# Another order of the steps in the engines' rounds, in the first phase of a two-layer decoder kernel

## The reference

```python
x = x + attention0(layernorm(x))          # rotary-like: cos and sin of table angles, 16 heads, causal softmax
x = x + cross0(layernorm(x), ctx)         # 16 heads, scores clipped at +-10000, softmax, no mask
x = x + experts0(layernorm(x))            # router: softmax of 16 logits, argmax, place in the expert's queue
...                                       # layer 1: attention, cross attention, quantised feed-forward
```

## Time and profile before

| | us |
|---|---|
| median of 3 runs | 3380.1 (3377.64 to 3380.84) |
| the profiled execution | 3377.66 |
| its span, first to last instruction | 3375.9 |

### The profile page before, as it was taken

The page is one execution under the profiler, slowest core; times in us unless marked ns, Lnnn a source line. Parts: engine busy times, 40 slices in busy tenths (PEclk is TensorE's granted clock), DMA queues, the critical chain, the costliest instruction groups (busy, mean ns, idle before and its releaser), DMA issues. The chain is left out here.

```text
span 3375.9 us, 57669 instructions
## 1 busy us (share of the span) xinstructions
PE 3101.4 (92%) x21302; PEld 2150.3 (64%) x21302; DVE 2328.1 (69%) x4781; ACT 1799.4 (53%) x3243; POOL 1295.6 (38%) x1933
## 2 busy tenths in 40 slices
PE   3899999999999998699999786899999999999997
PEld 2566666666666665466666453576766667666764
DVE  3588888888888887242111484687888877888774
ACT  3788788888788874211111132555555555555552
POOL 4366666666666663100000351233333333333322
PEclk8899999999999999799999897999999999999998
DMA  5877777878777873333333253433433434433420
GB/s 99 149 119 107 105 109 108 112 101 110 104 107 108 108 99 48 118 117 117 117 104 123 78 168 80 64 62 58 68 60 56 62 59 67 63 56 59 62 39 13
DMA packets 291102, 301.17 MB, mean 89 GB/s; under 512 B 35243, under 2 KB 278427, under 8 KB 290821
## 3 DMA queue, kind: packets, MB, share of 16 engines
q1 hardware_dynamic: 276420, 273.41, 48.4%
q0 software_dynamic: 6144, 15.68, 1.6%
q10 hardware_dynamic: 8256, 8.39, 0.8%
HBM read 95.51 MB, written 50.40 MB: 43 GB/s over the span
## 5 line engine op out<-in xcount | busy, mean ns | idle before, releaser
L493 DVE TENSOR_REDUCE xa_mx<-bank 128x2 f32<-128x512 f32 x1024 | 670.5, 688 | 151.8 <-PE bank L483 146.5
L597 ACT ACTIVATE xa_p<-bank 128x512 f32<-128x512 f32 x1024 | 568.5, 599 | 310.6 <-PE bank L587 305.4
L608 DVE SCALAR_TENSOR_TENSOR xa_p<-xa_p,bank 128x1024 f32<-128x1024 f32 x256 | 306.6, 1217 | 38.4 <-PE bank L576 23.4
L933 POOL TENSOR_SCALAR_AFFINE_SELECT xa_p<-xa_p 128x256 f32<-128x256 f32 x512 | 201.7, 406 | 222.1 <-ACT xa_p L924 209.8
L620 PE MATMUL bank<-xa_p,xa_v 128*32 128x256 f32 x4096 | 277.3, 389 | 1.7 <-DVE xa_p L608 1.4
L924 ACT ACTIVATE xa_p<-bank 128x384 f32<-128x384 f32 x512 | 236.9, 492 | 54.3 <-PE bank L912 36.0
L1952 POOL DMA_INDIRECT sa_y<-expert_out,sa_s x64 | 70.1, 1095 | 508.2 <-POOLq L1853 482.5
L1747 ACT ACTIVATE ex_h<-bank,ex_b 128x512 f32<-128x512 f32 x64 | 44.0, 687 | 361.7 <-PE bank L1736 361.7
L1736 PE MATMUL bank<-ex_xt,ex_w 128*128 128x512 f32 x512 | 224.6, 597 | 0.7 <-ACT ex_xt L1727 0.7
L1766 PE MATMUL bank<-ex_w,ex_h 128*128 128x256 f32 x1024 | 224.0, 379 | 1.0 <-issue 0.9
L587 PE MATMUL bank<-ex_w,xa_ks 99*128 99x256 bf16 x1024 | 183.9, 277 | 30.5 <-ACT xa_p L597 22.2
(11 more groups left out here) (284 smaller groups left out, 6849.1 us busy)
## 6 DMA issues: line engine op xcount, KB each, us to landing
ex_w<-ra_parts SPq DMA_DIRECT2D x384, 128.0 KB, 6.6
xa_ks<-xa_pk SPq DMA_DIRECT2D x384, 128.0 KB, 4.6
ex_w<-in_L_ffn_W SPq DMA_DIRECT2D x32, 1024.0 KB, 7.2
xa_qs<-xa_pq SPq DMA_DIRECT2D x192, 128.0 KB, 4.7
ex_w<-xa_pq SPq DMA_DIRECT2D x192, 128.0 KB, 4.6
ra_x<-in_x SPq DMA_DIRECT2D x32, 256.0 KB, 8.1
xa_ctx<-in_ctx_t SPq DMA_DIRECT2D x64, 128.0 KB, 3.9
queue<-zeros ACTq DMA_DIRECT2D x4, 2048.0 KB, 7.9
```

Of the source, the lines that this page charges most:

```text
L493: c.nc.vector.tensor_reduce(c.xa.row_max[:, :, n], halves(c.banks[2 + n % 2]), AX.X, ALU.max).then_inc(s.max_taken, 1)
L597: c.nc.scalar.activation(c.xa.p_beside[:, n // 2 % 4, :, n % 2, :], halves(c.banks[n % 2]), ACT.Exp, scale=SCALE).then_inc(s.exp, 1)
L608: c.nc.vector.scalar_tensor_tensor(out=p, in0=p, scalar=1.0, in1=c.banks[bank][:, :].unsqueeze(1).broadcast_to([P, TC, 2 * S]), op0=ALU.mi ...
L933: c.nc.gpsimd.affine_select(out=diagonal, in_=diagonal, compare_op=ALU.is_ge, fill=0.0, base=0, pattern=[[0, TC], [1, P]], channel_multipl ...
```

## The change

The slots of the first phase are others; no step is added, dropped or changed, and the rounds keep their lengths. Much of it moves a step by one place among steps that don't touch it. In the steady round these steps stand elsewhere:

- TensorE: the rotary turn is behind cross score 1 (was behind cross score 9). Rotary sum 2 is behind the turn of the rows (was ahead), the first turn of the rotary sums is ahead of the turn of the rows. Cross values are behind max 7 (were behind max 4). Queries are ahead of max 0; floor 7 is behind the rotary values and ahead of cross sum 2.
- VectorE: the first cross normalisation is ahead of max 0 (was behind max 2). Some neighbours swap.
- ScalarE: the rotary values' copy is behind the cross floor (was behind cross exp 7); the queries' middle part behind rotary exp 1 (was behind exp 7); the high parts behind rotary exp 3 (were behind exp 1); the keys' middle part behind cross exp 10.
- GpSimd: the router's place and then the rotary power stand between masks 7 and 8 (place was ahead of mask 0, the power between the two low parts); the queries' low part is behind mask 0 (was behind mask 8); masks 14 and 15 are behind the split; the indirect rows are behind the second low part.
- SyncE: the stack of the queries goes ahead of the row of maxima; context behind the rotary stacks.

```diff
@@ pe_phase_a
-        for b, _ in due(n, period, (567,)):
+        for b, _ in due(n, period, (550,)):
             pe_ra_turn(c, b)
-        for b, k in due(n, period, (691, 696, 706, 708)):
+        for b, k in due(n, period, (691, 696, 708, 709)):
             pe_ra_sum(c, b, k)
-        for b, _ in due(n, period, (749,)):
+        for b, _ in due(n, period, (747,)):
             pe_xa_queries(c, 6, c.wx, b)
-        for b, _ in due(n, period, (757,)):
+        for b, _ in due(n, period, (763,)):
             pe_xa_values(c, 6, c.wx, b)
...
@@ dve_phase_a
-        for b, _ in due(n, period, (465,)):
+        for b, _ in due(n, period, (461,)):
             dve_xa_normalise(c, b, 0)
...
@@ act_phase_a
-        for b, _ in due(n, period, (373,)):
+        for b, _ in due(n, period, (376,)):
             act_ra_high(c, b)
-        for b, _ in due(n, period, (407,)):
+        for b, _ in due(n, period, (390,)):
             act_ra_values(c, b)
-        for b, _ in due(n, period, (485,)):
+        for b, _ in due(n, period, (477,)):
             act_xa_middle_q(c, b)
...
@@ pool_phase_a
-        for b, _ in due(n, period, (166,)):
+        for b, _ in due(n, period, (181,)):
             pool_ra_power(c, b)
-        for b, k in due(n, period, (231, 232, 234, 235, 236, 237, 238, 239, 240, 242, 243, 244, 245, 246, 247, 249)):
+        for b, k in due(n, period, (228, 230, 231, 232, 234, 235, 236, 237, 240, 241, 242, 243, 244, 245, 247, 248)):
             pool_ra_mask(c, b, k)
-        for b, _ in due(n, period, (270,)):
+        for b, _ in due(n, period, (258,)):
             pool_xa_low_q(c, b)
-        for b, _ in due(n, period, (306,)):
+        for b, _ in due(n, period, (304,)):
             pool_xa_split_both(c, b)
-        for b, _ in due(n, period, (344,)):
+        for b, _ in due(n, period, (354,)):
             pool_rt_place(c, b)
-        for b, _ in due(n, period, (345,)):
+        for b, _ in due(n, period, (369,)):
             pool_rt_rows(c, d["queue"], b)
...
```

More of the change, by code:

```diff
@@ L1322, in pe_phase_a @@
             pe_xa_turn_out(c, b)
-        for b, _ in due(n, period, (950,)):
+        for b, _ in due(n, period, (949,)):
             pe_a_project(c, 6, b)
-        for b, _ in due(n, period, (968,)):
+        for b, _ in due(n, period, (969,)):
             pe_rt_turn(c, 0, b)
-        for b, _ in due(n, period, (972,)):
+        for b, _ in due(n, period, (973,)):
             pe_rt_logits(c, 3, b)
@@ L1341, in dve_phase_a @@
             dve_ra_index(c, b)
-        for b, _ in due(n, period, (362,)):
+        for b, _ in due(n, period, (361,)):
             dve_ra_normalise(c, b, 0)
@@ L1345, in dve_phase_a @@
             dve_ra_normalise(c, b, 1)
-        for b, _ in due(n, period, (365,)):
+        for b, _ in due(n, period, (364,)):
             dve_xa_rest_k(c, 6, c.wx, b)
@@ L1353, in dve_phase_a @@
             dve_xa_normed(c, c.ra.x1[b % 4], b)
-        for b, _ in due(n, period, (382,)):
+        for b, _ in due(n, period, (383,)):
             dve_xa_rest_q(c, 6, c.wx, b)
-        for b, k in due(n, period, (420, 421, 422, 425, 426, 427, 428, 430, 431, 432, 433, 434, 435, 436, 437, 438)):
+        for b, k in due(n, period, (421, 422, 423, 425, 426, 427, 428, 430, 431, 432, 433, 434, 435, 436, 437, 438)):
             dve_xa_max(c, b, k)
@@ L1359, in dve_phase_a @@
             dve_xa_bound(c, b)
-        for b, k in due(n, period, (446, 448, 449, 453, 455, 458, 459, 460)):
+        for b, k in due(n, period, (447, 448, 449, 453, 455, 458, 459, 460)):
             dve_xa_clip(c, b, 2 * k)
-        for b, _ in due(n, period, (465,)):
+        for b, _ in due(n, period, (461,)):
             dve_xa_normalise(c, b, 0)
@@ L1367, in dve_phase_a @@
             dve_a_end(c, 6, b)
-        for b, _ in due(n, period, (484,)):
+        for b, _ in due(n, period, (485,)):
             dve_rt_stats(c, b)
@@ L1377, in act_phase_a @@
     period = ROUND_A["act"]
-    for n in range((B - 1) * period + 620):
-        for b, _ in due(n, period, (358,)):
+    for n in range((B - 1) * period + 618):
+        for b, _ in due(n, period, (355,)):
             act_ra_xn_t(c, b)
@@ L1414, in act_phase_a @@
             act_xa_raw(c, b, 0)
-        for b, _ in due(n, period, (579,)):
+        for b, _ in due(n, period, (580,)):
             act_xa_raw(c, b, 1)
@@ L1420, in act_phase_a @@
             act_rt_xn_t(c, 0, b)
-        for b, _ in due(n, period, (619,)):
+        for b, _ in due(n, period, (617,)):
             act_rt_exp(c, b)
@@ L1460, in sp_phase_a @@
     period = ROUND_A["sp"]
-    for n in range((B - 1) * period + 63):
-        for b, _ in due(n, period, (3,)):
+    for n in range((B - 1) * period + 68):
+        for b, _ in due(n, period, (2,)):
             sp_ra_load(c, x_rows[b], b)
-        for b, _ in due(n, period, (20,)):
+        for b, _ in due(n, period, (23,)):
+            sp_ra_stack(c, b, 0)
+        for b, _ in due(n, period, (24,)):
+            sp_ra_stack(c, b, 1)
+        for b, _ in due(n, period, (25,)):
             sp_xa_context(c, d["ctx_t"][b], b)
[L1466 to L1469, removed]
+        for b, _ in due(n, period, (36,)):
+            sp_xa_stack_k(c, b)
         for b, _ in due(n, period, (37,)):
-            sp_xa_stack_k(c, b)
-        for b, _ in due(n, period, (40,)):
             sp_xa_stack_q(c, b)
-        for b, _ in due(n, period, (47,)):
+        for b, _ in due(n, period, (46,)):
             sp_xa_max_rows(c, b)
-        for b, _ in due(n, period, (62,)):
+        for b, _ in due(n, period, (67,)):
             sp_a_end(c, x2_rows[b], b)
```

62 lines of the change are left out of this document (31 added, 31 removed).

## The result

The changed kernel takes 3381.97 us (median of 20 runs, 3379.93 to 3391.84); the kernel before, on the same chip beside it, 3376.88 us (20 runs, 3370.96 to 3380.84). The ratio is 1.002, 95% interval 1.0014 to 1.0027: slower by about 5 us, where 20 were forecast. The profiled execution took 3381.32 us.

The account below looks back on a forecast made before the run. No engine is full; a loop of handoffs through four in-order queues sets the 39.22 us round. 35.15 + 4.86 = 40.01 a round, 0.79 x 27 - 0.7 = +20.6 us, gave a median of 3400, range 3388 to 3412.

Parts of the forecast that it names:

- X to the eighth rotary exp: Stretch from X through the first rotary exp (X+21.5) to the eighth, forecast at X+27.7, bounds of second part 5.8 to 6.5.
- X: Start of an item's first cross-attention exp on ScalarE; times in the round are counted in us behind it.
- GpSimd from mask 7 to the split: Masks 8 to 13 wait behind place (2.02) and power (0.70), delaying the split; row turn at X+35.15 against X+34.90.
- The other path: Row maxima and bound on VectorE: bound at X+31.9, turn possible at X+34.3, but GpSimd 0.8 later, so gain lost.
- Row turn to the next first exp: Sums 2 and 3 and keys all behind TensorE's row turn: 4.86 us against 4.32, bounds 4.75 and 5.0.
- The filling: First rounds hang on the load and the index chain, whose orders stay: +-3 us.
- The sum: Round of 35.15 + 4.86 = 40.01 against 39.22, for 27 rounds, the last without the power: +20.6 us.
- A: Rival, chance 0.14: GpSimd's block is hidden, the row's transfer path still decides, round 39.4; time 3380 to 3386.
- B: Rival, chance 0.11: new order wins, floor path decides, split reached before X+33; round 38.7, -14 us, 3366.
- C: Rival, chance 0.20: block weighs more (long cast 0.49 extra, eighth exp at 6.5, masks 2.4); round +1.7, 3426.
- D: Rival, no chance given: the change is only a relabelling, order in the steady round the same.

## Why the prediction was right in its mechanism and wrong in its size

**X to the eighth rotary exp.** Right. First rotary exp at X+21.39 (taken 21.5), eighth at about 643.16, X+27.53 (27.7).

**GpSimd from mask 7 to the split.** Right, and it decides. Place starts at X+28.58 (27.7 + 0.55 + 0.37 = 28.62), block 1.98 (2.02, with the cast of 0.19), power 0.69 (0.70), masks 2.49 (2.25; its bound "at most 2.4" was too low), split to turn 1.39 (1.55). Row turn at X+35.13, forecast X+35.15. That it agrees to 0.02 is in part luck: the masks' +0.24 and the split's -0.16 cancel for the most part, and the rest goes against the other terms.

**The other path.** Right: bound at X+31.76 (31.9). "This gain is lost" is right as well, and what is lost is much, 0.84 a round against the kernel before: without the block the turn follows the bound by 2.25 instead of 3.37, and the round is 38.42.

**Row turn to the next first exp.** This step failed, by the size of its terms: 4.44 us, not 4.86, and below its own lower bound of 4.75. The releaser is the one forecast (the high part of the keys, and the exp right behind it). Its terms were read off starts in the kernel before: 0.36 from turn to sum, 0.79 for a sum, 2.03 from the keys to their high part, 0.84 and 0.05 for the high part and the issue. Measured are 0.24, 1.44 for both sums together, 2.03, and 0.73 from the high part to the exp. The 0.36 held a wait: in the kernel before it is sum 3 that follows the turn, and its weights wait for GpSimd's mask 15, which stands behind the split:

```profile
652.40 0.59 PEld L620 LDWEIGHTS bank<-xa_p,ra_v 128*32 128x32 f32 x16 [0.19 <-POOL xa_p L933]
```

The 0.79 is a sum's time ahead of the keys; ahead of another sum it is 0.68, and ahead of the keys 0.76 here. And an ACTIVATE's listed duration (0.84 for two) is longer than what the next one waits for (0.73). That is 0.12 + 0.14 + 0.16 = 0.42 a round, 11 us of the miss in 27 rounds.

**The base.** One round of before was read, 39.22; the mean is 39.256. Another 1 us.

**The filling.** This step failed too: +-3 with "whose orders stay"; measured -4.85. The order did not stay: the power left its place between the low parts, and that alone gives 4.1 where it was tried by itself (180.46 to 176.40). The changed kernel moves it further, behind mask 7, and its share there was not taken apart. The prediction had this edit, and weighed it only in the steady round.

**The sum.** Forecast 0.79 x 27 - 0.7 = +20.6. Off this come 0.49 x 26 = 12.7 for the round (+0.30 measured for +0.79) and 4.9 for the filling, and 3.0 is left; with the 0.7 of the tail that is the +3.7 of the spans.

**The rivals.** A had the time (3380 to 3386) and not the mechanism: it needed GpSimd's block to be hidden and the transfer path to decide, and the trace shows neither. B said that the new order wins if the split is reached before X+33. Its condition failed here (649.37, X+33.74), and where an experiment made it true its 38.7 was even too high (38.42). C's long cast did not come (186 to 187 ns, 18 of 18); of its other terms the masks were longer than its 2.4, the eighth exp earlier than its 6.5. D is refuted by place's price of 1.14 a round.

The Trainium skill ("SBUF — State Buffer", Who interferes with whom) says that a tensor_reduce on VectorE never contends with GpSimd on trn2, by which the cast beside reduces is short. This case's trace agrees: 0.19 in all 32 items of the changed kernel.

## What to carry to other kernels

When an in-order queue has no wait left between its input and a hand-over, every instruction in that stretch counts in full (the power, 0.70 us long, cost 0.72); with slack it is free (0.00). So ask first which engine is late at the hand-over, and price the move in both cases. A releaser has to be looked up in the trace even where the size came out: two expectations here had the size nearly right and the path wrong. And check that a moved slot lands where you say: two positions in a round were named wrongly here, and one of them changed what the experiment tested. Take terms of a new sequence from groups that already run back to back, not from the spacing of starts that may hold a wait. A table of a pipeline has a filling too: an instruction of no price in the steady round can stand in the first items' chain, and there it adds up from item to item (0.7 us long, 4.1 us in all).

## What the runs showed beyond that

- A small GpSimd operation beside VectorE's index wrap (L862) takes 0.65 to 0.75 instead of 0.18 to 0.20, in 26 of the 32 items of each kernel where one starts beside it. In the kernel before it is the cast; in the three kernels with place early made from the changed one it is L1238, a TENSOR_TENSOR on 128x2. GpSimd and VectorE of the kernel with place and power early and sum 2 ahead:

```profile
621.87 0.74 POOL L1238 TENSOR_TENSOR rt_over<-rt_over,rt_base 128x2 f32<-128x2 f32 x1
622.68 0.18 POOL L1241 CAST rt_i<-rt_over 128x2 int32<-128x2 f32 x1
```

```profile
621.87 0.69 DVE L862 TENSOR_SCALAR ra_sine<-ra_sine 128x1024 int32<-128x1024 int32 x1
```

- The last rounds don't run at one clock. In both kernels the granted clock is 1.00 from 180 to 1200 us. TensorE is busy 9.6 of the 10 us from 1290 in both; from 1310 it is busy 6.3 of 10 us before and 5.2 after, and there the granted clock falls and then changes between its two levels, 1.2 and 2.4 GHz, not at the same times in the two kernels. Windows of before, then of after:

```profile
1320.00:1340.00 20.00, 16.92 (x146) 9.06 (x144) 14.99 (x27) 8.90 (x17) 4.23 (x13) 0.89 0.21 32
```

```profile
1320.00:1340.00 20.00, 17.69 (x105) 10.59 (x106) 11.45 (x20) 9.16 (x17) 3.37 (x13) 0.59 0.02 7
```

The last round takes 40.52 instead of 34.95, and still the way from the 28th turn to the end is only 0.7 longer. How much of the 40.52 is the clock was not taken apart.
- Rounds that wait for the transfer of the row scatter: 39.17 to 39.49 before, 38.74 to 39.09 with place and power early and sum 2 ahead. Most kernels without that wait repeat within 0.1 (39.53 to 39.62 changed, 38.41 to 38.47 with place and power early). Single rounds stand out in three of them: 39.38 among 39.0 to 39.07 with TensorE's and ScalarE's order, 39.07 among 38.69 to 38.76 with the low part early and without VectorE's order, 38.66 with the power moved.
